# A two-layer transformer and a mixture of experts on one core: eleven step durations changed in the planner's table

## The chip, the cores and the metric

One Trainium2 chip, one of its cores. The metric is the time of one execution of the whole program on that core, in microseconds (us). Three runs of the kernel before give a median of 3349.57 us (3342.55 to 3351.56).

## What is computed

Eight sequences of 512 tokens of width 256 (`x`) and as many contexts go through two layers. The reference, cut to what matters:

```python
# layer 0, 16 heads of 16, quantised attention; _fq rounds to 8 bits
h1 = _ln(x);  x = _attn(h1, h1, a1_*) + x            # stage 0
h2 = _ln(x);  x = _attn(h2, context, a2_*) + x       # stage 1
h3 = _ln(x);  a, g = split(h3 @ ff_w1 + ff_b1)       # stage 2
x = a * gelu(g) @ ff_w2 + ff_b2 + x
# in _attn: out = einsum(_fq(softmax(_fq(q) @ _fq(k).T * SCALE)), _fq(v)) @ wo + bo
# layer 1, exact attention
x = _layernorm(x + _attn(x, x, x, sa_*, causal=True))        # stage 3
x = _layernorm(x + _attn(x, enc, enc, ca_*, causal=False))   # stage 4
x = _layernorm(x + _moe(x))     # 8 experts, 2 per token     # stages 5, 6, then experts
```

## The kernel before

`build` (its last part) runs two programs after each other: `transformer`, the stages 0 to 6 for all eight batches, and `experts`, the mixture of experts, the last normalisation and the output. The change touches the first alone.

The transformer is cut into some 12,000 **steps**, each a tuple `(kind, B, s, n)`: a kind of work, the batch, the stage, a number. `program_steps` (L245) names for each step what it must follow. `ON` (L93) puts each kind on one engine. `program_order` (L498) is a list scheduler that runs while the kernel is being built: it plays the steps through with planned durations, takes again and again the step that could begin first (within `AHEAD`, 0.05 us, the one with the longest way to the end, `to_end`), and writes the list `ORDER`. Every engine then issues its own steps in the order of that list and waits on semaphores for what each needs. So the planned durations change no instruction and no semaphore rule; they set only the order in which each in-order engine takes its steps, which bank of PSUM (6 or 7) a projection gets, and where fillers go.

The planned durations are `TAKES` (L111), `takes` (L159) for kinds with several sizes, `LANDS` for DMAs from issue to landing, `HOP` and `TAIL` for what lies between engines. **Fillers**: where the plan leaves PE idle for `WARM_GAP` (0.4 us) or more and a bank is idle, `program_order` puts in steps `W` (L1462), products of an identity that nobody reads, so that PE does not stand still.

The kinds that the text speaks of:

- Quantised attention (stages 0 and 1), 32 units of two heads each: `S` scores on PE (L1564, two products), `M` row maximum on DVE (L1293), `nb` (L1296), `E` exponential on ACT (L1429, two per unit), `R` reciprocal on DVE (L1299), `Q` on POOL (L1096), `T` eight transposes on PE (L1572), `ev` on DVE (L1305), `AV` on PE (L1584).
- Exact attention (stages 3 and 4): `A` scores on PE (L1595) whose row maxima `am` DVE takes (L1313), `ms` and `MT` (L1604) and `mt` (ACT, L1437), which put the maxima as rows under q; then `B` the shifted scores (L1617), `E2` their exponential on ACT (L1448, L1450), `AV2` (L1634), `n1` (DVE). `A` and `B` read q and k as stacks of bfloat16 parts, `kst` and `qst`. A stack is made by a round trip through DRAM: `spk` / `spq` split on POOL (L1104 to L1110), `psk` / `psq` store the parts (SP, L970), `pkk` / `pkq` load them again in six DMAs (SP, L983). Each stack comes in two halves: the first is needed by `A` number 0, the second by `A` number 32.
- Projections and feed-forward: `xT`, `cT` transposes (L1503), `k`, `q` (L1519), `v` (L1515), `y` (L1532), `g` and `w` (L1542, 16 steps each), `z` (L1553). `dg` drains `g` on ACT (L1411), and `ge` is the GELU over all of it, two instructions on ACT (L1416); every `w` waits for it, by `("ge", B, 2, 0)` in its step.
- Weights stream through a ring of six pieces of 256 KB (`wring`, L910). SP issues the load of a piece at the place in `ORDER` where the last reader of the piece six before it stands. So a new order of projections also moves DMA issues on SP's queue, which is one line with the stores and loads of the stacks.

The exact attention of one batch runs beside the quantised attention and feed-forward of the next ones. Batches 1 to 6 repeat one pattern. Time in that pattern, for the texts below: stage 0 of batch 3 with the feed-forward of batch 2, then stage 3 of batch 2, then stage 1 of batch 3, then stage 4 of batch 2.

Of the kernel before, what the change touches and what calls it, by code (L numbers as in the profile page):

```python
# [71 lines left out]
def place_taken(B):  # L72
# [36 lines left out]
ROUTING_OPENS = ("A", 6, 3, 0)  # L109
AHEAD = 0.05  # L110
TAKES = {"LR": 0.5, "rT": 0.49, "dr": 0.66, "rL": 1.95, "rl": 0.64, "rx": 0.25, "rm": 1.4, "ry": 0.25, "ri": 3.6, "rP": 0.36, "rp": 1.4, "sc": 1.1,  # L111
# [3 lines left out]
         "ki": 0.46, "qi": 0.45, "vi": 0.4, "psk": 0.5, "psq": 0.5, "pkk": 2.7, "pkq": 2.7,  # L115
         "dy": 0.6, "g": 0.88, "dg": 0.62, "ge": 6.4, "w": 0.9, "dw": 0.65, "z": 0.97, "dz": 0.6,
         "bi": 0.7, "gb": 1.53, "ST": 0.5, "LX": 0.5, "LC": 0.5, "st": 0.88, "rs": 1.4, "xn": 0.53}
TAIL = {"PE": 0.13, "DVE": 0.08, "ACT": 0.08, "POOL": 0.0, "SP": 0.0}
HOP = {"PE": 0.12, "DVE": 0.06, "ACT": 0.06, "POOL": 0.09, "SP": 0.3}
# [1943 lines left out]
```

## Time and profile before

| | |
|---|---|
| median of three runs | 3349.57 us |
| the profiled execution's own time | 3340.18 us |
| its span | 3338.4 us, 59062 instructions |
| PE / DVE / ACT / POOL busy | 2940.4 / 2165.5 / 1959.5 / 1625.8 us (88 / 65 / 59 / 49%) |
| mean granted TensorE clock | 0.947 |
| DMA | 344.05 MB, 103 GB/s over the span |
| number of GELU table loads and GELUs on ACT | 8 and 16 |

The busy time of PE is modelled and counts overlapping matmuls, so PE looks busier than it is. "issue" as a releaser means that the engine waited for nothing that the profile shows: a DMA's semaphore is often such a case. The transformer ends at about 2745 us, and the experts take the rest.

### The profile page before, as it was taken

What the parts mean: (1) busy time and instruction counts of PE and PEld (TensorE: products, weight loads), DVE (VectorE), ACT (ScalarE), POOL (GpSimd) and SP (SyncE); (2) the same over time, 40 slices, a digit from 0 to 9 for tenths busy, and PEclk for the clock granted to TensorE, in tenths of its full rate; (3) what the DMA queues carried; (4) which work ended last, traced back from release to release, by engine and by line L of the source; (5) the groups of instructions that cost most, each with busy time, mean ns of one, the idle gap of its engine ahead of it and who ended that gap; (6) DMA issues with size and microseconds to landing.
All of it is one profiled execution on the core that took longest, in us unless ns stands there. A gap on an engine that the chain in (4) does not pass through costs nothing. (4 is left out here: it accounts for less than half of the span.)

```text
span 3338.4 us, 59062 instructions
## 1 busy us (share of the span) xinstructions
PE 2940.4 (88%) x19111; PEld 1705.4 (51%) x19111; DVE 2165.5 (65%) x4580; ACT 1959.5 (59%) x4178; POOL 1625.8 (49%) x2835
## 2 busy tenths in 40 slices
PE   6888999899998898989999989987988859999991
PEld 3445443544454354435443544454435229999991
DVE  4887796788678787967896788778656511111115
ACT  3666667576758676675767576757354404444442
POOL 4665572675367366726763664457435321111115
PEclk9999999999999999999999999997999879999996
DMA  3002331422142214303320422141433239999995
GB/s 95 17 23 65 65 63 32 86 61 56 34 96 51 51 42 92 71 26 83 71 54 24 90 44 61 29 86 36 107 79 85 46 83 326 326 325 327 324 327 164
DMA packets 295832, 344.05 MB, mean 103 GB/s; under 512 B 33262, under 2 KB 273006, under 8 KB 295328
## 3 DMA queue, kind: packets, MB, share of 16 engines
q1 hardware_dynamic: 287376, 323.35, 36.7%
q0 software_dynamic: 6480, 17.58, 1.6%
q8 instruction: 133, 2.18, 0.3%
q14 instruction: 115, 0.94, 0.1%
q10 hardware_dynamic: 1728, 0.01, 0.0%
HBM read 291.50 MB, written 51.23 MB: 103 GB/s over the span
## 5 line engine op out<-in xcount | busy, mean ns | idle before, releaser
L1429 ACT ACTIVATE probs<-ps,nbias,sc 128x512 f32<-128x512 f32 x1024 | 789.9, 777 | 270.1 <-DVE nbias L1296 223.1
L1096 POOL TENSOR_SCALAR pq<-probs,rstep 128x512 f16<-128x512 f32 x1024 | 709.7, 693 | 232.9 <-PE ps L1572 147.9
L1313 DVE TENSOR_REDUCE m<-ps 128x1 f32<-128x512 f32 (+3 forms) x1024 | 560.7, 582 | 249.4 <-PE ps L1598 128.8
L1293 DVE TENSOR_REDUCE nmax<-ps 128x2 f32<-128x1024 f32 x512 | 620.3, 1212 | 85.9 <-PE ps L1564 85.4
L1595 PE MATMUL ps<-kst,qst 96*128 96x512 bf16 (+3 forms) x1024 | 330.2, 354 | 77.2 <-issue 39.9
L1305 DVE TENSOR_SCALAR big<-ps 128x1024 bf16<-128x1024 f16 x512 | 348.1, 680 | 61.6 <-PE ps L1572 60.1
L1906 ACT ACTIVATE hT<-moe_ps,e_b 128x128 f32<-128x128 f32 x568 | 208.3, 367 | 281.4 <-PE moe_ps L1860 242.2
L1572 PE MATMUL ps<-id,pq 128*128 128x128 f16 x4096 | 328.1, 226 | 47.5 <-DVE big L1305 40.5
L1617 PE MATMUL ps<-qst,kst 108*128 108x512 bf16 (+3 forms) x1024 | 304.5, 351 | 66.2 <-ACT big L1448 29.5
L1572 PEld LDWEIGHTS ps<-id,pq 128*128 128x128 f16 x4096 | 258.5, 100 | 190.7 <-issue 124.6
L1448 ACT ACTIVATE big<-ps 128x512 f32<-128x512 f32 (+3 forms) x640 | 272.9, 482 | 134.4 <-PE ps L1620 83.4
L1812 POOL DMA_INDIRECT rows_out<-yb,words x71 | 69.9, 984 | 472.8 <-DVE yb L1991 472.8
L1984 DVE COPY words<-moe_in 128x3 uint32 x71 | 12.0, 169 | 432.4 <-PE moe_ps L1882 432.4
L1542 PE MATMUL ps<-xT,wring 128*128 128x512 f32 x512 | 270.5, 636 | 0.3
L1860 PEld LDWEIGHTS moe_ps<-moe_bT,e_w 128*128 128x128 f32 x2272 | 266.1, 193 | 5.5 <-issue 2.0
L1860 PE MATMUL moe_ps<-moe_bT,e_w 128*128 128x128 f32 x2272 | 266.5, 276 | 1.8 <-DMA e_w<-in_L_xattn_e_w_dram 1.8
L1882 PE MATMUL moe_ps<-e_w,hT 128*128 128x256 f32 x1136 | 256.8, 380 | 0.0
L1595 PEld LDWEIGHTS ps<-kst,qst 96*128 96x128 bf16 x1024 | 98.1, 99 | 303.2 <-DVE m L1313 178.1
L1564 PE MATMUL ps<-kmask,qi 32*128 32x512 bf16 x1024 | 203.7, 397 | 40.2 <-ACT probs L1429 27.7
L1462 PE MATMUL ps<-idb 128*128 128x512 bf16 x777 | 215.9, 393 | 26.0 <-DVE sc L1144 19.8
L1634 PE MATMUL ps<-big,v_f 128*32 128x512 f32 (+3 forms) x2048 | 234.5, 535 | 2.6 <-ACT big L1448 0.8
L1882 PEld LDWEIGHTS moe_ps<-e_w,hT 128*128 128x128 f32 x1136 | 210.8, 191 | 25.3
(219 smaller groups left out, 4671.8 us busy)
## 6 DMA issues: line engine op xcount, KB each, us to landing
e_w<-in_L_xattn_e_w_dram SPq DMA_DIRECT2D x142, 1024.0 KB, 7.5
wring<-in_L_xattn_ff_w_dram SPq DMA_DIRECT2D x96, 256.0 KB, 2.8
parts<-parts_sb SPq DMA_DIRECT2D x64, 384.0 KB, 2.6
kst<-parts SPq DMA_DIRECT2D x192, 128.0 KB, 4.5
qst<-parts SPq DMA_DIRECT2D x192, 128.0 KB, 5.0
moe_in<-rows_in SPq DMA_DIRECT2D x71, 140.0 KB, 2.6
xn<-in_ctx_dram SPq DMA_DIRECT2D x16, 512.0 KB, 3.8
got<-rows_out SPq DMA_DIRECT2D x16, 512.0 KB, 6.8
```

The lines of the kernel that those rows point to most:

```text
L1096: nc.gpsimd.tensor_scalar(pq[:, u % 2, h, :], probs[:, u % 2, h, :], rstep[:, u % 2, h:h + 1], HALF_ROUND, ALU.mult, ALU.add).then_inc(SIG ...
L1293: nc.vector.tensor_reduce(nmax[:, n % 2, :], ps[:, a:a + 2, :], AX.X, ALU.max, negate=True).then_inc(SIG["M"], 1)
L1305: nc.vector.tensor_scalar(probs_t[:, g % 2, 2 * p:2 * p + 2, :, t * P:(t + 1) * P], PT, -HALF_ROUND, WMAX, ALU.add, ALU.min).then_inc(SIG[ ...
L1313: nc.vector.tensor_reduce(m32[:, g % 2, t, h:h + 1], bank(("A", B, s, n))[:, 0:width], AX.X, ALU.max, negate=True).then_inc(SIG["am"], 1)
L1429: nc.scalar.activation(probs[:, u % 2, h, :], ps[:, BANKS[("S", B, s, u)][h], :], ACT.Exp, bias=nbias[:, u % 2, h:h + 1], scale=sc[:, s:s ...
L1448: last = nc.scalar.activation(ex[:, half, h, j, i0:N], ps[:, from_, i0:N], ACT.Exp, scale=SCALE)
L1542: last = nc.tensor.matmul(bank(e), wt[:, k, (f % 2) * P:(f % 2 + 1) * P], xT[:, k, :], start=(k == 0), stop=(k == KT - 1))
L1572: last = nc.tensor.transpose(PT[:, h, j, :], pq[:, n % 2, h, j * P:(j + 1) * P], id16[:, :])
L1595: last = nc.tensor.matmul(bank(e)[:, 0:width], qst[0:PAIR_ROWS, head, t * P:(t + 1) * P], kst[0:PAIR_ROWS, head, 0:width], start=True, sto ...
L1617: last = nc.tensor.matmul(dst[:, i0:N], kst[0:rows_, head, jt * P:(jt + 1) * P], qst[0:rows_, head, i0:N], start=True, stop=not causal(s))
L1860: last = nc.tensor.matmul(ps[:, HIDDEN_BANK[f % banks], 0:BLOCK], w1[:, slot, k, f * P:(f + 1) * P], bT[:, slot % 2, k, :], start=(k == 0) ...
L1882: last = nc.tensor.matmul(ps[:, 2 + 2 * slot + s, 0:D], hT[:, slot, f, s * P:(s + 1) * P], w2[:, ws, f, :], start=(f == 0), stop=(f == FT ...
```

## The change

Eleven numbers of `TAKES` are replaced: `S`, `M`, `T`, `MT`, `xT`, `cT`, `dc`, `k`, `q`, `ki` and `ge`. Nothing else differs in the source.

```diff
-         "W": 0.22, "S": 0.38, "M": 1.14, "nb": 0.14, "E": 0.76, "R": 0.08, "T": 0.46, "ev": 0.61, "AV": 0.23, "do": 0.6,
-         "ms": 1.1, "MT": 0.32, "mt": 0.95, "n1": 0.92, "n2": 0.6, "n3": 0.62,
-         "xT": 0.49, "dT": 0.66, "cT": 0.44, "dc": 0.5, "k": 0.88, "q": 0.88, "v": 0.97, "dv": 0.6, "dV": 0.6,
-         "ki": 0.46, "qi": 0.45, "vi": 0.4, "psk": 0.5, "psq": 0.5, "pkk": 2.7, "pkq": 2.7,
-         "dy": 0.6, "g": 0.88, "dg": 0.62, "ge": 6.4, "w": 0.9, "dw": 0.65, "z": 0.97, "dz": 0.6,
+         "W": 0.22, "S": 0.32, "M": 1.17, "nb": 0.14, "E": 0.76, "R": 0.08, "T": 0.5, "ev": 0.61, "AV": 0.23, "do": 0.6,
+         "ms": 1.1, "MT": 0.1, "mt": 0.95, "n1": 0.92, "n2": 0.6, "n3": 0.62,
+         "xT": 0.52, "dT": 0.66, "cT": 0.55, "dc": 0.48, "k": 0.92, "q": 0.92, "v": 0.97, "dv": 0.6, "dV": 0.6,
+         "ki": 0.6, "qi": 0.45, "vi": 0.4, "psk": 0.5, "psq": 0.5, "pkk": 2.7, "pkq": 2.7,
+         "dy": 0.6, "g": 0.88, "dg": 0.62, "ge": 3.73, "w": 0.9, "dw": 0.65, "z": 0.97, "dz": 0.6,
```

The new `ORDER` holds the same work with 779 fillers where there were 777. Of the 4304 steps of PE that are no fillers, 3251 stand at another place than before, most of them by a few places; of DVE's 3584 steps 1785 do, of ACT's 2200 steps 1194, of POOL's 1832 steps 860.

SP's queue, batch 2, before the first `A` of stage 3. `wring` is a weight piece, `parts<-parts_sb` a store of parts (`psk` or `psq`), `kst<-parts` and `qst<-parts` the loads of the stacks (`pkk`, `pkq`). Before:

```order
L910 DMA wring<-in_L_xattn_a_wo_dram 128x2x256
L970 DMA parts<-parts_sb 128x3x512 x2
L910 DMA wring<-in_L_xattn_ca_wq_dram 128x2x256
L983 DMA kst<-parts 16x8x512 x6
L910 DMA wring<-in_L_xattn_ca_wv_dram 128x2x256
L983 DMA qst<-parts 16x8x512 x6
L910 DMA wring<-in_L_xattn_a_wq_dram 128x2x256
L910 DMA wring<-in_L_xattn_ca_wk_dram 128x2x256
L970 DMA parts<-parts_sb 128x3x512
```

Now:

```order
L910 DMA wring<-in_L_xattn_a_wo_dram 128x2x256
L970 DMA parts<-parts_sb 128x3x512
L983 DMA kst<-parts 16x8x512 x6
L910 DMA wring<-in_L_xattn_a_wq_dram 128x2x256
L970 DMA parts<-parts_sb 128x3x512
L910 DMA wring<-in_L_xattn_ca_wq_dram 128x2x256
L983 DMA qst<-parts 16x8x512 x6
L910 DMA wring<-in_L_xattn_ca_wk_dram 128x2x256
L910 DMA wring<-in_L_xattn_ca_wv_dram 128x2x256
L970 DMA parts<-parts_sb 128x3x512
```

The store and the load of k's stack now stand ahead of the store of q's parts, and between that store and the load of q's stack there is one weight piece, where there were two pieces and the load of k's stack.

ACT around the GELU of batch 2 (`uT<-uT`). `uT<-ps,ffb` is `dg`, `qst<-ps` is `mt`, `probs` is `E`, `big` is `E2`. Before:

```order
L1411 ACTIVATE uT<-ps,ffb 128x512
L1416 ACT_TABLE_LOAD
L1416 ACTIVATE uT<-uT 128x2048 x2
L1437 ACTIVATE qst<-ps 12x1024
L1429 ACT_TABLE_LOAD
L1429 ACTIVATE probs,rsum<-ps,nbias,sc 128x512
L1448 ACTIVATE big<-ps 128x512
L1429 ACTIVATE probs,rsum<-ps,nbias,sc 128x512
L1448 ACTIVATE big<-ps 128x512
L1429 ACTIVATE probs,rsum<-ps,nbias,sc 128x512
```

Now:

```order
L1448 ACTIVATE big<-ps 128x512
L1429 ACTIVATE probs,rsum<-ps,nbias,sc 128x512
L1448 ACTIVATE big<-ps 128x512
L1437 ACTIVATE qst<-ps 12x1024
L1429 ACTIVATE probs,rsum<-ps,nbias,sc 128x512
L1448 ACTIVATE big<-ps 128x512
L1429 ACTIVATE probs,rsum<-ps,nbias,sc 128x512 x2
L1411 ACTIVATE uT<-ps,ffb 128x512
L1416 ACT_TABLE_LOAD
L1416 ACTIVATE uT<-uT 128x2048 x2
L1448 ACT_TABLE_LOAD
L1448 ACTIVATE big<-ps 128x512
```

The GELU with its two table loads stood ahead of both `mt` of the last head group of stage 4; now it stands behind both, behind six `E` and behind four `E2`. On PE the last two `g` steps moved from ahead of the second `S` to behind the first `T`, and the first `w` from behind the fourth `S` to behind the seventh.

## Rows read from the trace of the kernel before

**Rows 1.** Windows: stretch, length; busy PE, PEld, DVE, ACT, POOL; clock, DMA share, GB/s.

```profile
0.00:2745.00 2745.00, 2423.68 (x15561) 1218.43 (x15561) 2033.15 (x4199) 1713.71 (x3506) 1514.96 (x2716) 0.95 0.27 60
...
850.40:1160.60 310.20, 282.91 (x1867) 143.62 (x1866) 245.45 (x482) 212.24 (x435) 179.82 (x327) 0.97 0.29 60
850.40:871.00 20.60, 13.37 (x55) 5.38 (x54) 11.18 (x22) 18.55 (x32) 6.92 (x13) 0.75 0.05 12
...
946.50:953.50 7.00, 1.04 (x6) 0.38 (x5) 0.00 (x0) 3.23 (x7) 5.28 (x7) 0.78 1.14 195
...
1004.30:1029.30 25.00, 21.02 (x159) 9.30 (x160) 20.62 (x41) 22.95 (x56) 20.63 (x37) 0.93 0.18 43
```

**Rows 2.** Waits of PE, transformer only: total us, times, longest.

```profile
PE ps L1595 <- issue: 39.9, 10, 8.1
...
PE ps L1617 <- ACT qst L1437: 28.3, 11, 4.1
```

**Rows 3.** Timeline of PE around the first score product of batch 2.

```profile
945.31 1.88 PE L1519 MATMUL ps<-xT,wring 128*128 128x512 f32 x4
953.15 0.26 PE L1595 MATMUL ps<-kst,qst 96*128 96x128 bf16 x1 [5.96 <-issue]
```

**Rows 4.** Timeline of DVE, the same place.

```profile
953.56 0.51 DVE L1313 TENSOR_REDUCE m<-ps 128x1 f32<-128x128 f32 x2 [7.25 <-PE ps L1598]
```

**Rows 5.** Timeline of SP's queue, the same place.

```profile
934.44 1.49 SPq L970 DMA_DIRECT2D parts<-parts_sb  x2
...
938.65 2.79 SPq L983 DMA_DIRECT2D kst<-parts  x6
...
942.01 2.78 SPq L983 DMA_DIRECT2D qst<-parts  x6
```

**Rows 6.** Timeline of ACT around the GELU of batch 2.

```profile
848.15 0.69 ACT L1411 ACTIVATE uT<-ps,ffb 128x512 f32<-128x512 f32 x1 [1.89 <-PE ps L1542]
848.86 1.28 ACT L1416 ACT_TABLE_LOAD   x1
850.15 3.71 ACT L1416 ACTIVATE uT<-uT 128x2048 f32<-128x2048 f32 x2
853.89 1.02 ACT L1437 ACTIVATE qst<-ps 12x1024 bf16<-12x1024 bf16 x1
854.92 1.28 ACT L1429 ACT_TABLE_LOAD   x1
```

**Rows 7.** Timeline of PE, the same place.

```profile
850.45 0.39 PE L1564 MATMUL ps<-kmask,qi 32*128 32x512 bf16 x2
854.96 0.61 PE L1617 MATMUL ps<-qst,kst 108*128 108x512 bf16 x1 [4.12 <-ACT qst L1437]
857.72 0.58 PE L1617 MATMUL ps<-qst,kst 108*128 108x512 bf16 x1 [2.15 <-ACT big L1448]
...
866.61 0.39 PE L1617 MATMUL ps<-qst,kst 108*128 108x512 bf16 x1
```

**Rows 8.** SP's queue before the first score product of another stage.

```profile
769.38 0.37 SPq L970 DMA_DIRECT2D parts<-parts_sb  x1
771.91 2.70 SPq L983 DMA_DIRECT2D qst<-parts  x6
```

**Rows 9.** Page, DMA issues: count, KB each, median us from issue to landing.

```profile
qst<-parts SPq DMA_DIRECT2D x192, 128.0 KB, 5.0
```

**Rows 10.** SP's queue, second stacks of batch 2.

```profile
963.72 0.38 SPq L970 DMA_DIRECT2D parts<-parts_sb  x1
969.73 2.83 SPq L983 DMA_DIRECT2D qst<-parts  x6
```

**Rows 11.** Instructions by line and form: count, busy us, mean ns.

```profile
L1429 ACT ACTIVATE probs<-ps,nbias,sc 128x512 f32<-128x512 f32 x1024 | 789.9, 777 | 270.1 <-DVE nbias L1296 223.1 <-POOL pq L1096 44.7
...
L1448 ACT ACTIVATE big<-ps 128x512 f32<-128x512 f32 x256 | 153.4, 599 | 75.0 <-PE ps L1617 47.3 <-PE ps L1620 24.2 <-PE ps L1634 1.3
```

**Rows 12.** Timeline of PE at the start of stage 1 of batch 3.

```profile
1010.79 0.39 PE L1564 MATMUL ps<-kmask,qi 32*128 32x512 bf16 x2 [2.30 <-ACT probs L1429]
```

## The prediction

> **What bounds the kernel now.** Read the windows first [rows 1]. The transformer takes the first 2745 us of the span; the change cannot touch the rest. Batches 1 to 6 repeat a pattern of 310.20 us, in which DVE is busy 245.45 us, ACT 212.24, POOL 179.82, and PE 282.91 by a modelled figure that counts overlaps. No engine fills the pattern alone: PE and DVE take turns as the bound, and what a new order can win is the stretches where both stand. Two of them show. In 850.40 to 871.00 DVE works 11.18 us of 20.60 and the granted clock is 0.75. In 946.50 to 953.50 DVE works not at all, PE 1.04 us of 7.00, at a share of 1.14 on the DMA engines. A third is milder: 1004.30 to 1029.30 has DVE at 20.62 of 25.00.
>
> The waits of PE [rows 2] name them. `A` waited ten times, 39.9 us, for something that the profile does not show. `B` waited eleven times, 28.3 us, for the rows of maxima that ACT copies (`mt`), 4.1 us at most.
>
> The first: PE ends q's projection for stage 3, then stands 5.96 us before the first `A` [rows 3], and DVE stands 7.25 us [rows 4]. SP's queue says why [rows 5]: the parts of k and q are stored from 934.44 on, k's stack is loaded from 938.65, q's only from 942.01, over 2.78 us, and `A` starts when its last piece is there, at 953.15. Of the ten waits six are this one, in batches 1 to 6 (the other four are smaller or at the two ends). They leave 39.9 as an upper bound for all, and six times 5.96 is 35.8; I use 36.
>
> The second: ACT loads a table for GELU (1.28 us), runs it (3.71), copies maxima (1.02), then loads the table for the exponential (1.28) [rows 6]. PE issued its `S` at 850.45, waits 4.12 for the copy and 2.15 for an `E2` behind the second load [rows 7]. This too comes once in each of six batches.
>
> **The change part by part.** No instruction but fillers is added or removed, so every term is a wait that goes, comes or moves. Each is for one batch of the pattern and counts six times; the sum is made against the profiled execution's 3340.2 us.
>
> *q's stack.* In the new list SP stores q's parts behind k's stack load, and one weight piece stands between that store and the load of q's stack. The nearest row of such a chain alone is that of another stage: store at 769.38, load of q's stack from 771.91 to 774.61 [rows 8], and 5.0 us for a piece to land [rows 9], so 10.2 us from store to landing, where here it took from about 935.2 (the second store of the pair at 934.44) to 953.15, 18 us [rows 3, 5]. Against that stands the work that PE has between the store and the first `A`. Going through the new list it is four `S`, four `T`, three `v`, two `q` steps and one `k`, 8.6 us; before it was 10.6, and 10.6 + 6.0 is 1.4 short of the 18: that much PE waits for other things there. Now 10.2 - 8.6 - 1.4 is nearly nothing; as the k stack and one more piece are on the same DMA engines, I leave a wait of 1.5. Minus 4.5, times six: **-27**. Bounds: the wait goes wholly (-36), or nothing is won (0; the rival below goes past it).
>
> *The second half of q's stack*, needed by the 33rd `A`. Before, its parts were stored at 963.72 and, behind k's stack on the DMA engines, took until 969.73, where the load began [rows 10]; with 2.83 us of issuing and 5.0 to land [rows 9] it was there at about 977.6, 24.4 us after the first `A` and ahead of its use by little. Nothing in the new list makes this chain shorter, but the 33rd `A` now stands some 4.5 us of PE work nearer to the first (a `y` pair, `B` steps and one `AV2` moved behind it). DVE's row maxima slow PE there and give part of it back, so I take a new wait of 1.5 us: **+9**. Bounds 0 and +4 each (+24).
>
> *The GELU.* The new value 3.73 is the two instructions' 3.71 us without the two table loads of 1.28 beside them; the old 6.4 was 3.71 + 2 x 1.28 = 6.27 with both [rows 6]. So the planner now thinks ACT free 2.6 us before it is. By hand from rows, counted from the second `S` of the new stage: ACT does six `E` of 0.78, four `E2` of 0.60 [rows 11], one `mt` of 1.02 and one `dg` of 0.69, 8.8 us with 0.8 of waiting; then 6.27 us of GELU and loads, then the `E2` that frees the bank of the next `B`: that `B` comes at +16.5. Before it was 866.61 - 850.45 = 16.2 [rows 7]. The long wait is not removed, it moves from the 25th `B` to the 30th. Until then PE has done two `g`, a `T` and a `cT` more and two `w` less. Then ACT owes six `E` and four `E2`, 7.1 us, for which PE has 4.6 us of work, as the first `w` comes late. I set 2.0 us slower: **+12**. Bounds: 1.5 faster (-9), when PE catches up while DVE bounds it; 4 slower (+24).
>
> Here a page speaks against the change. The trace shows a load of 1.28 us, and the first GELU starts 0.01 us after it [rows 6]. The Trainium skill, page "ScalarE: Activation LUTs", section "What ACT_TABLE_LOAD costs", gives 1283 ns for the load and about 1380 ns more for a drain, 2.66 us for each switch; by that the two switches would be 5.3 us, and the planner would be 2.7 us further off in each batch, some 16 us over six, which would take this sum to about nothing. The trace agrees with the load and shows no drain ahead of the GELU, so the sum goes by 1.28.
>
> *Start of stage 1.* PE waited 2.30 us for an `E` at 1010.79 [rows 12], and DVE's idle share from 1004.30 to 1029.30 is 4.4 us in 25. In the new list the products of q and the `E` stand ahead of the normalisation on POOL, and k's projection of stage 4 (four steps) stands later, where fillers stood. DVE is then the bound and can win at most the idle time above that of its packed stretches: I take 1.5 us: **-9**. Bounds 0 and 3 (-18).
>
> *Everything else* (the other thousands of neighbours that changed places): nothing, because DVE or PE has no gap over 1 us beside them. *Two more fillers*: nothing, at most 0.4 us each, and they stand where PE idles. First and last batch: nothing, with 8 us to either side in the range; there fewer fillers stand ahead of the last stage 4, and chains of single steps set the time.
>
> **The sum**: -27 + 9 + 12 - 9 = -15 us, 3325 us for the execution profiled. That execution is 9.4 us under the median of the runs. Scaled to the median: 3349.6 - 15 = **3334.5 us**. A measurement of this kernel can tell some 0.3%, 10 us, from no change, so the forecast is just past that line.
>
> **The rivals.**
>
> *Slower: q's stack lands as late as it did, counted from its use.* Mechanism: the load of q's stack is issued with 6.0 us of PE work ahead of the first `A`, before it had 6.5, and the store of q's parts queues behind k's stack, as it did there (6.0 us from 963.72 to 969.73, where the same store alone took 2.5 [rows 8, 10]). For it: exactly this queueing stands in the trace. Against: in the new list k's stack is issued some 5 us of PE work before q's store, so most of it is through. If the chain from store to landing is 16 us instead of 10.2, it is shortened only by the 2 us that the cover lost, and the wait stays at 6.0. From there on it decides: with nothing won at the first `A` the rest is 9 + 12 - 9 = +12, **3362 us**.
>
> *Same: the GELU eats the win.* ACT's backlog is not made good before the next stage, since PE is full from 871 to 946: 4 us per batch instead of 2, or the second half of q's stack waits 3 us. Then -15 + 12 = -3, **3347 us**. A drain of 1.38 us at each switch, which no row shows, would end here too (-15 + 6 x 2.7 = +1, 3350 us): chance 0.03 of the 0.27; the rule is the Trainium skill's, as above.
>
> *Same, in another way*: the order is not what bounds the pattern; whatever wait is taken from PE, DVE's 245 us with its own chains give it back. Against it: in both big holes DVE stands too. It gives 3350 us.
>
> **How the numbers follow.** Forecast and its like (faster by more than 10 us): 0.52. Slower by more than 10 us, the first rival above all: 0.21. The cases that end within 10 us: 0.27 (the GELU 0.17, the drain 0.03, the order without effect 0.07). The best corner that I believe (first wait gone, GELU even) is 15 + 9 + 12 + 6 = 42 us: 3307, with a little for the ends 3306. The upper end is the first rival with 0.8 us more at each second half, 3366. The range leaves out 2 in 10.
>
> **What would show it.** In the profile after: the wait of `A` on "issue" well under 39.9 us in total, under 20, with a hole in DVE ahead of the first `A` of under 3 us; on SP's queue k's stack load ahead of q's store. At the 33rd `A` a wait that was not there. ACT: the two table loads and the GELU behind six `E`, and one wait of `B` on `big` of about 5 us instead of 4.12 on `qst` and 2.15; the sum of waits of `B` on `qst` down by 25 us and on `big` up by more. It is wrong if the pattern of 310.2 us is not 2 to 3 us shorter, if `A`'s waits stay, or if the time changes mainly in the first batch or the last 400 us.

## The result, and the profile after

The changed kernel takes **3412.12 us** (median of four runs, 3406.90 to 3432.70); the kernel before, run beside it, 3346.06 (3341.36 to 3351.56). The ratio is **1.0202**, 95% interval 1.0183 to 1.0221: 66 us slower. The forecast was 3334.5, and its range ended at 3366. The execution profiled took 3417.22 us at a span of 3415.4 and a clock of 0.930, against 3340.18 and 0.947 before.

The windows of the changed kernel, columns as in [rows 1]:

```profile
0.00:2825.00 2825.00, 2484.01 (x15563) 1238.67 (x15563) 2054.03 (x4200) 1719.73 (x3506) 1523.89 (x2716) 0.93 0.27 58
...
868.90:1193.70 324.80, 292.03 (x1867) 146.34 (x1866) 249.23 (x482) 212.81 (x434) 181.11 (x327) 0.94 0.28 58
1193.70:1514.60 320.90, 290.57 (x1868) 144.59 (x1867) 249.10 (x482) 212.89 (x434) 181.25 (x327) 0.95 0.28 58
```

The same work, 1867 matmuls and 482 instructions of DVE, takes 321 to 325 us per batch where [rows 1] had 310.20. ACT is busy as long as before, DVE 4 us longer. PE is busy 8 to 9 us longer with as many matmuls, at a clock of 0.94 to 0.95 instead of 0.97, and stands 30 to 33 us instead of 27. So the loss is a few us in which PE stands, and more in which it works at the lower clock around them.

PE's waits in the transformer of the changed kernel, columns as in [rows 2]:

```profile
PE ps L1617 <- ACT big L1448: 53.4, 69, 3.2
PE ps L1564 <- ACT probs L1429: 40.8, 80, 3.6
...
PE ps L1595 <- issue: 33.3, 11, 9.4
...
PE ps L1617 <- ACT qst L1437: 9.5, 16, 1.1
...
PE ps L1595 <- DMA qst<-parts: 4.9, 5, 1.5
```

Against [rows 2], `B`'s waits for `mt` fell from 28.3 to 9.5 us, and `A`'s for its stack only from 39.9 to 33.3. What grew are the waits for `E2`, 53.4 us, and for `E`, 40.8, both ACT's: these two rows stood at 29.5 and 27.7 us before.

ACT around the GELU of batch 2, which answers to [rows 6]:

```profile
879.66 0.69 ACT L1411 ACTIVATE uT<-ps,ffb 128x512 f32<-128x512 f32 x1 [0.23 <-PE ps L1542]
880.36 1.28 ACT L1416 ACT_TABLE_LOAD   x1
881.66 3.71 ACT L1416 ACTIVATE uT<-uT 128x2048 f32<-128x2048 f32 x2
885.38 1.28 ACT L1448 ACT_TABLE_LOAD   x1
886.68 0.60 ACT L1448 ACTIVATE big<-ps 128x512 f32<-128x512 f32 x1
```

And PE beside it, which answers to [rows 7]:

```profile
883.66 0.61 PE L1572 MATMUL ps<-id,pq 128*128 128x128 f16 x8 [2.08 <-DVE big L1305]
887.42 0.58 PE L1617 MATMUL ps<-qst,kst 108*128 108x512 bf16 x1 [3.15 <-ACT big L1448]
888.78 0.59 PE L1617 MATMUL ps<-qst,kst 108*128 108x512 bf16 x1 [0.78 <-ACT big L1448]
```

The block of 6.3 us on ACT is as foreseen, and the waits at it, 2.08 + 3.15 us, are even shorter than the 4.12 + 2.15 of [rows 7]. Whoever looks only at the wait that the change moves finds nothing wrong. The windows show where the loss is:

```profile
870.00:882.00 12.00, 8.35 (x45) 3.82 (x40) 7.46 (x15) 11.08 (x21) 4.06 (x9) 0.86 0.09 23
882.00:895.00 13.00, 6.46 (x31) 1.41 (x31) 4.93 (x9) 12.09 (x20) 4.47 (x8) 0.63 0.01 1
895.00:931.00 36.00, 35.20 (x193) 18.18 (x190) 27.76 (x52) 19.82 (x47) 15.74 (x30) 0.99 0.11 30
```

For 25 us ACT is full (11.08 of 12, 12.09 of 13) and PE has 14.8 us of work; then for 36 us PE is full and ACT has 19.8. The work that could have covered the first stretch stands in the second.

**Where the time went.** From the starts of named steps, mean of batches 1 to 5, in us. "w" is the time from the first `S` of stage 0 to the first `w`; the columns after it are the stretches S(0,0) to S(0,16), on to the first `A` of stage 3, to S(1,0), to S(1,16), to the next S(0,0), and their sum.

```
kernel                             w    S0-S16   to A   to S1  S1-S16  to S0    sum
before                           14.3    53.8    50.9    51.0    42.1  112.6   310.4
changed                          28.7    62.9    46.9    55.4    45.9  111.6   322.7
e1  changed, ge 6.4              12.4    53.4    47.1    52.0    46.0  112.5   311.0
e2  before, ge 3.73              28.8    62.6    51.5    53.0    42.8  114.2   324.1
e3  before, MT 0.1               14.3    54.1    51.6    52.4    43.0  112.8   314.0
e4  before, landing 5.0          12.2    57.1    43.5    48.8    42.8  114.4   306.7
e5  before, w held               24.2    57.7    50.7    53.5    43.1  112.6   317.6
e6  before, no table loads       11.7    51.3    50.9    51.3    42.5  112.5   308.5
e7  changed, no table loads      26.1    60.1    46.8    55.3    45.0  111.6   318.8
e8  e1, landing 5.0              12.1    58.1    44.6    52.1    43.6  111.5   310.0
e9  e1, context early            12.4    53.7    46.5    52.6    41.8  115.8   310.4
e10 changed, GELU pinned         11.6    53.1    46.6    52.0    43.7  112.8   308.2
e11 before, landing 4.0          12.7    54.6    45.5    50.0    43.2  114.4   307.7
e12 e9, landing 4.0              12.6    54.9    44.7    50.8    43.1  114.6   307.9
e13 changed, ge 4.2              20.2    57.9    46.6    56.2    45.3  112.0   318.1
e14 e10, landing 4.5             11.5    57.3    44.7    51.6    41.1  114.6   309.3
```

The table is made of five batches. Between the two profiled executions lie 77 us, and the same step starts divide them: five times 12.3, 62 us, from S(2,0,0) to S(7,0,0), the stretches of the table; 11 us from S(1,0,0) to S(2,0,0) (321.1 and 331.9), where the exact attention of batch 0 runs; and 4 us behind them. The 11 us of the first batch stay with the GELU put back (333.6 in e1, 334.4 in e10) and do not come with ge alone (323.1 in e2): they belong to the other ten values, not to the GELU.

A second caution: the borders of the stretches are steps, and a new order also moves work over them. In the changed kernel two `g` that stood ahead of S(0,0) stand behind it, and in e4 S0-S16 holds 13 steps of `z` where it held 7. Only the sum is free of that. The profiled execution of the kernel before lies 5 to 16 us under its own medians (3346 to 3357 in the sets below), so differences of 1 to 1.5 us a batch between two rows of this table are not resolved; where they matter the ratio of the runs decides.

### The profile page after: what moved, and what is told of

It reads as the page before. It is cut to its first block and busy times, and to the rows that moved or that the text cites. A ratio compares the mean times of both kernels' runs of the same rounds, so it can differ in the third digit from the quotient of the medians.

```text
span 3415.4 us, 59059 instructions
## 1 busy us (share of the span) xinstructions
PE 3001.9 (88%) x19113; PEld 1726.5 (51%) x19113; DVE 2186.1 (64%) x4580; ACT 1965.8 (58%) x4178; POOL 1633.7 (48%) x2835
## 5 line engine op out<-in xcount | busy, mean ns | idle before, releaser
L1595 PE MATMUL ps<-kst,qst 96*128 96x512 bf16 (+3 forms) x1024 | 330.7, 354 | 65.9 <-issue 33.3
L1617 PE MATMUL ps<-qst,kst 108*128 108x512 bf16 (+3 forms) x1024 | 314.5, 362 | 73.3 <-ACT big L1448 53.4
L1572 PEld LDWEIGHTS ps<-id,pq 128*128 128x128 f16 x4096 | 265.6, 102 | 179.3 <-issue 95.2
L1634 PE MATMUL ps<-big,v_f 128*32 128x512 f32 (+3 forms) x2048 | 250.8, 576 | 11.9 <-ACT big L1448 10.9
L1564 PE MATMUL ps<-kmask,qi 32*128 32x512 bf16 x1024 | 206.9, 403 | 52.7 <-ACT probs L1429 40.8
L1462 PE MATMUL ps<-idb 128*128 128x512 bf16 x779 | 222.9, 402 | 25.7 <-DVE sc L1144 19.8
L1092 POOL TENSOR_TENSOR rstep<-rinv,inv_step 128x2 f32<-128x2 f32 x512 | 103.1, 201 | 294.5 <-DVE rinv L1299 285.8
```

The lines of the kernel that those rows point to most:

```text
L1572: last = nc.tensor.transpose(PT[:, h, j, :], pq[:, n % 2, h, j * P:(j + 1) * P], id16[:, :])
L1595: last = nc.tensor.matmul(bank(e)[:, 0:width], qst[0:PAIR_ROWS, head, t * P:(t + 1) * P], kst[0:PAIR_ROWS, head, 0:width], start=True, sto ...
L1617: last = nc.tensor.matmul(dst[:, i0:N], kst[0:rows_, head, jt * P:(jt + 1) * P], qst[0:rows_, head, i0:N], start=True, stop=not causal(s))
```

## The experiments

Each ratio is to the kernel before, run beside it. The theories after the result: the loss is a few single places, the GELU's above all; against it, that any new order of this list loosens the cover everywhere.

**e1: ge put back.**

```diff
-         ... "ge": 3.73, ...
+         ... "ge": 6.4, ...
```

> The changed kernel with one value put back: ge 6.4 instead of 3.73. ACT then takes the GELU right behind dg 7 and ahead of the first E of the next stage, as before, while k of stage 4 stays six units of S later, as in the changed kernel. Theory P (the loss is in single places, the GELU's the largest): the stretch from S(B+1,0,0) to S(B+1,0,16) goes back from 61 to about 54 us, some 8 us x 7 batches, so about 3356 us; the start of stage 1 stays 4 us too long. Theory Q (the loss belongs to no place: any new order loosens the cover everywhere and the clock falls): 3395 to 3410.

Measured: 3352.63 us, ratio 1.0002 (0.9989 to 1.0015). The stretch S0-S16 is back at 53.4 us, the start of stage 1 stays at 46.0, both as the theory of single places has it. The other ten values together are worth nothing, within 5 us. That is a net: by the profiled executions they win 3.8 us a batch on the way to the first `A`, and lose 3.9 at the start of stage 1 and 12 in the first batch. The mean clock does not tell the time by itself: the twelve executions of e1 show 0.932 to 0.939 and those of the kernel before beside it 0.943 to 0.946, and the times are the same.

**e2: ge changed alone, in the kernel before.**

```diff
-         ... "ge": 6.4, ...
+         ... "ge": 3.73, ...
```

> The kernel before with one value changed: ge 3.73. The GELU moves behind four of the first E steps, w behind the sixth S; k of stage 4 stays where it was. Theory P: 8 us x 7 batches on top, about 3400 us, all of it between S(B+1,0,0) and S(B+1,0,16). Theory Q: 3350 to 3360, since the rest of the order is still the old one. My forecast's own term (+2 us a batch) would give 3360.

Measured: 3410.91 us, 1.0175 (1.0162 to 1.0188). One number makes 61 us, and its first stretch, 62.6 us, is within 0.3 us that of the changed kernel. The theory that any new order loses falls with e1, the forecast's +2 us with this one.

**e3: MT changed alone.**

```diff
-         "ms": 1.1, "MT": 0.32, ...
+         "ms": 1.1, "MT": 0.1, ...
```

> The kernel before with one value changed: MT 0.1. The GELU stays ahead of the first E; k of stage 4 moves from the third to behind the ninth S of stage 1. Theory P: start of stage 1 (S 0 to S 16) 4 to 5 us longer in each batch, about 3376 us, the rest unchanged. Rival: k late costs nothing there, since fillers and ACT's queue set the pace, and the 4 us of the changed kernel come from something else: 3346 us.

Measured: 3357.22 us, 1.0023 (1.0013 to 1.0033): 8 us slower, where theory P had 3376 us and the rival no loss. S1-S16 is 43.0 us. k of stage 4 is now as late as in the changed kernel (22.4 us after S(1,0), changed 24.1, before 10.6) and costs about 1 us there, not 4. The rival is nearer: k's lateness alone is not the +3.8 us.

**e4: the landing time of the stacks.**

```diff
-LANDS = {..., "psk": 2.2, "psq": 2.2, "pkk": 2.2, "pkq": 2.2, ...}
+LANDS = {..., "psk": 5.0, "psq": 5.0, "pkk": 5.0, "pkq": 5.0, ...}
```

> The kernel before with the landing time of the four stack DMAs planned at 5.0 us instead of 2.2; no duration changed. k and q of stage 3 move two to three units of S earlier. Theory P: the wait ahead of A(B,3,0), 6.0 us in the kernel before, falls under 1.5 us and nothing else moves much: 3346 - 5 x 7 = about 3311 us. Rival: k and q taken earlier leave PE without cover at the end of stage 0, or the first S units lose it: 3340 to 3355.

Measured: 3324.01 us, 0.9929 (0.9916 to 0.9942): faster than both kernels. Waits of `A` in it:

```profile
PE ps L1595 <- DVE m L1313: 32.5, 115, 0.7
...
PE ps L1595 <- DMA qst<-parts: 2.5, 3, 1.1
...
PE ps L1595 <- issue: 1.7, 1, 1.7
```

39.9 us on "issue" have become 1.7. The rival is partly right too: 7.4 us a batch are won on the way to the first `A` and 2.2 behind it, and 3.3 lost in S0-S16 and 1.8 in the last stretch; into S0-S16 the new order moves six steps of `z`. That is why 26 us came and not 35.

**e5: w held back, the GELU left in its place.** Also "ge" 4.5 and `E(B+1,0,3)`, the fourth exponential, behind `ge`; in the list that these make, the GELU of batches 1 to 6 stands ahead of the first `E` and the first `w` behind the seventh `S`, where e2 has it.

```diff
-                step("w", ..., ("ge", B, 2, 0), k and ("w", B, 2, 2 * f))
+                step("w", ..., ("ge", B, 2, 0), k and ("w", B, 2, 2 * f),
+                     f == 0 and k == 0 and B + 1 < NBATCH and ("S", B + 1, 0, 4))
```

> The kernel before with the GELU kept right behind dg 7 and ahead of the first E, as it was there, but with w forbidden to start until S(B+1,0,4) is done, so that the first w comes behind the sixth S, where the kernel with ge 3.73 alone has it (before: behind the third). Nothing of ACT's work is moved to speak of. Theory C (w and z are the PE work that covers ACT's long queue of E and E2, and their delay is the loss, wherever the GELU stands): S 0 to S 16 takes 60 to 62 us and the kernel 3390 to 3410. Theory B (the loss is ACT's block of 6.3 us falling in the middle of the running E pipeline instead of ahead of it): 54 to 55 us, and 3346 to 3355.

Measured: 3381.87 us, 1.0075 (1.0057 to 1.0093): between the two. S0-S16 is 57.7 us: 3.9 of e2's 8.8 us. Theory B, which gave at most 55, falls as the whole story; theory C gave 60 to 62 and is right in kind, too large in size. The windows of batch 3 from the first `S` to the first `w`, and from there to S 16, say where e2 differs. The kernel before, then e5, then e2:

```profile
848.00:862.30 14.30, 7.07 (x41) 2.28 (x40) 5.90 (x11) 14.00 (x19) 3.05 (x6) 0.74 0.06 19
862.30:901.90 39.60, 39.54 (x218) 18.99 (x216) 32.71 (x60) 27.59 (x65) 19.88 (x39) 0.96 0.10 28
```

```profile
860.00:883.90 23.90, 15.48 (x90) 5.72 (x86) 14.00 (x25) 23.27 (x42) 8.71 (x17) 0.71 0.04 12
883.90:917.20 33.30, 32.98 (x178) 16.51 (x174) 25.59 (x45) 17.61 (x42) 14.59 (x27) 1.00 0.11 32
```

```profile
862.60:888.90 26.30, 16.50 (x85) 5.50 (x84) 12.06 (x22) 23.61 (x40) 8.22 (x16) 0.77 0.05 15
888.90:923.70 34.80, 34.80 (x186) 17.00 (x184) 27.26 (x49) 19.01 (x46) 15.28 (x30) 0.98 0.12 31
```

In all three PE is full from the first `w` on (39.54 of 39.60, 32.98 of 33.30, 34.80 of 34.80), and before it ACT is nearly so, PE to a half or two thirds at a clock of 0.71 to 0.77. The first stretch is where time is lost: it grows by 9.6 and 12.0 us, and the second, with fewer matmuls left for it, shrinks by only 6.3 and 4.8. In e5 ACT is full to the last (23.27 of 23.90); in e2 it stands 2.7 us of the window, in a hole of 3.16 us ahead of its first `E` that begins before the window:

```profile
864.59 0.78 ACT L1429 ACTIVATE probs<-ps,nbias,sc 128x512 f32<-128x512 f32 x1 [3.16 <-DVE nbias L1296]
```

That is the time in which the first `S`, its row maxima and its bias pass through PE and DVE. ACT has nothing to do then, and in the kernel before the GELU stood there. Of the 4.9 us between e5 and e2 this hole may be a part; another is that e2 also has three `g` steps behind S 0 (0.88 us planned for each), which e5 has ahead of it. No run parts the two.

**e6 and e7: no table loads**, in the kernel before and in the changed one. Both leave out the GELU, so the output differs.

```diff
-                        nc.scalar.activation(part, part, ACT.Gelu)...
+                        nc.scalar.activation(part, part, ACT.Identity)...
```

> The kernel before with ACT.Identity in place of ACT.Gelu in L1416, so that the GELU is left out and with it the two table loads around it (the output differs). The loads are 2 x 1.28 us of ACT at a place where PE waits: 8 x 2.57 = 21 us less at most, about 3328 us; 3346 if something else ends those waits.

> The changed kernel with ACT.Identity in place of ACT.Gelu in L1416, so that the two table loads around each GELU are gone and 3.73 us is what it takes (the output differs). If the uncounted loads are the damage (theory L), this comes within 10 us of the run without loads of the kernel before. Theory C: the planner's place is a bad one even when its price is right, since it puts w and z behind ACT's queue either way; the difference to the other run stays over 40 us, this one about 3385 us.

Measured: 3339.53 us, 0.9955 (0.9940 to 0.9971), and 3388.83 us, 1.0110 (1.0093 to 1.0127). The two instructions are as long as GELU was (1904 ns in e7, 1902 in the changed kernel), so only the loads are gone. In S0-S16 that is 2.5 us in the one and 2.8 in the other, about 2 x 1.28. Over the whole kernel it is 15 us in e6 and, from the two ratios, some 31 in e7, around the 20.5 us that the sixteen loads last. The two runs stand 49 us apart, where the kernels with loads stand 66. So theory L falls as the main cause: 3.73 is the true time in e7, and the planner's place for it is still bad.

By the Trainium skill (page "ScalarE: Activation LUTs", section "What ACT_TABLE_LOAD costs"), which gives 2.66 us for each switch, an estimate for the two switches is 5.3 us. The rows of this case do not bear out the part beside the load: ACT's next instruction starts 0.02 us after each of the two loads at 880.36 and 885.38, and the stretch became shorter by the loads alone.

**e8: ge put back, and landing 5.0.** The edits of e1 and e4 in the changed kernel.

```diff
-         ... "ge": 3.73, ...
+         ... "ge": 6.4, ...
-LANDS = {..., "psk": 2.2, "psq": 2.2, "pkk": 2.2, "pkq": 2.2, ...}
+LANDS = {..., "psk": 5.0, "psq": 5.0, "pkk": 5.0, "pkq": 5.0, ...}
```

> The changed kernel with ge back at 6.4 and the landing of the four stack DMAs planned at 5.0 us instead of 2.2, that is, the run with ge put back (1.0002 of the kernel before) plus the change that alone gave 0.9929. If the two are additive: 3326 us, the wait ahead of A(B,3,0) under 1 us. If the ten new durations gained only by closing part of that same wait, which the landing time closes as well, their losses at the start of stage 1 (4 us a batch) stay and it is slower than that: 3335 to 3350.

Measured: 3346.23 us, 0.9967 (0.9954 to 0.9981). Not additive, as the second case had it. But the reason that I gave for it fails: against e4 the largest loss is 3.3 us between the first `A` and S(1,0), and in S1-S16 it is 0.8, not 4.

**e9: the context early**, in e1.

```diff
-            step("S", B, s, u, *(...), free)
+            step("S", B, s, u, *(...), free, u == 0 and s == 1 and B and ("cT", B - 1, 4, 1))
```

> The run with ge put back (e1), and in its planner one more condition: S(B+1,1,0) behind cT(B,4,1). That puts cT 1 of the context, and with it k of stage 4 (four matmul groups, 4 us of PE), back where the kernel before has them, k behind the third S of stage 1 instead of the ninth, and 11 fillers instead of 4 to 5 into S 0 to S 16. Theory K (the ten other values lose 4 us a batch at the start of stage 1 because its PE cover is gone and the granted clock falls there a second time, 15 to 25 us in, to 0.77 and 0.67): S 0 to S 16 goes from 46.0 to about 42 us, the clock stays at 1.0 in that stretch, and the kernel takes 3349 - 4 x 7 = about 3322 us. Rival: the same work is only moved out of that stretch into the next ones (y of stage 3 and AV2), as the run with MT alone suggests (+0.9 us): 3345 to 3352.

Measured: 3356.24 us, 0.9998 (0.9987 to 1.0010). Windows of e1, S(3,1,0) to S(3,1,16) and its part from 15 to 25 us:

```profile
1013.00:1058.80 45.80, 38.03 (x289) 19.61 (x285) 38.35 (x72) 35.24 (x87) 33.34 (x58) 0.89 0.21 39
1028.00:1038.00 10.00, 8.59 (x59) 3.74 (x58) 9.24 (x22) 8.28 (x22) 7.95 (x15) 0.83 0.00 0
```

and of e9:

```profile
1014.80:1056.60 41.80, 35.46 (x284) 17.03 (x283) 35.15 (x69) 35.60 (x87) 33.35 (x59) 0.92 0.19 36
1029.80:1039.80 10.00, 7.98 (x62) 3.40 (x61) 7.83 (x16) 9.90 (x24) 8.42 (x14) 1.00 0.10 28
```

The stretch is 4.2 us shorter and the clock in its part holds at 1.00, exactly as theory K says, and the kernel is no faster: the stretch behind it grew by 3.3 us. The low clock went there too. The next 40 us or so, in e1 and in e9:

```profile
1058.80:1098.50 39.70, 37.86 (x283) 19.91 (x283) 35.49 (x74) 30.59 (x71) 33.93 (x63) 1.00 0.34 63
1056.60:1100.50 43.90, 39.13 (x273) 22.23 (x271) 38.71 (x77) 30.56 (x70) 33.70 (x60) 0.92 0.32 63
```

Theory K falls, the rival holds. The loss, in work and in clock, was moved over a border that I had drawn.

**e10: all eleven values, the GELU pinned.**

```diff
-                step("E", B, s, 2 * u + h, ("nb", B, s, u), ...)
+                step("E", B, s, 2 * u + h, ("nb", B, s, u), 2 * u + h == 2 and s == 0 and B and ("ge", B - 1, 2, 0), ...)
```

> The changed kernel with all its eleven durations, ge 3.73 among them, and one more condition in the planner: E(B+1,0,2) behind ge(B). The GELU so comes right behind dg 7 and ahead of the first E again, with its price left at 3.73. If its place alone is the loss: S 0 to S 16 about 54 us, the same 3350 us as with ge put back. If the price does harm elsewhere too (it shortens every chain that passes over the GELU, and so changes whom the planner prefers): 3365 to 3400.

Measured: 3341.76 us, 0.9963 (0.9950 to 0.9975). The price stays wrong, only the place is forced (the GELU of batches 1 to 6 is ahead of the first `E` again), and the whole loss is gone and a little more. Its windows, as above:

```profile
860.70:872.30 11.60, 5.09 (x28) 1.79 (x27) 5.30 (x9) 11.47 (x16) 2.20 (x4) 0.72 0.02 6
872.30:913.80 41.50, 41.44 (x233) 20.50 (x230) 34.69 (x64) 28.70 (x68) 21.51 (x42) 0.95 0.09 26
```

The stretch to the first `w` is 11.60 us. The 12 us that it wins are not the ten values' alone, since with ge 6.4 they win nothing (e1); the kernel before with 3.73 and the pin, which would part them, was not run.

**e11 and e12: landing 4.0**, in the kernel before and in e9.

```diff
-LANDS = {..., "psk": 2.2, "psq": 2.2, "pkk": 2.2, "pkq": 2.2, ...}
+LANDS = {..., "psk": 4.0, "psq": 4.0, "pkk": 4.0, "pkq": 4.0, ...}
```

> The kernel before with the landing of the four stack DMAs planned at 4.0 us (5.0 gave 0.9929, 2.2 is the kernel before). The wait ahead of A(B,3,0), 8.8 us from S 31 before and 2.2 with 5.0, should be 3 to 4 us; what 5.0 cost on the other side (S 0 to S 16 up by 3.3 us, A(B,4,0) to A(B,4,63) up by 4.3) should be less. If these two trade evenly: 3325 to 3330 us; if the cost on the other side is mostly avoided: 3310 to 3320.

> The ten other new durations with ge at 6.4, the context kept early as in the run with S(B+1,1,0) behind cT(B,4,1), and the stack DMAs planned at 4.0 us. If the measured durations are worth something once the two bad places are out: under the run with landing 4.0 alone, 3300 to 3315 us. If the ten durations are neutral: the same as that run. If their orders conflict (849 fillers and 3346 us with landing 5.0, where additivity gave 3326): over it, 3330 to 3345.

Measured: 3337.19 us, 0.9943 (0.9929 to 0.9958), and 3336.16 us, 0.9953 (0.9935 to 0.9971). In e11 S0-S16 costs 0.8 us instead of 3.3 and the way to `A` gains 5.4 instead of 7.4: the two trade evenly. In e12 the ten values add nothing.

**e13: ge 4.2** in the changed kernel, which puts the GELU behind the second `E` and the first `w` behind the sixth `S` (the expectation counts from 0).

```diff
-         ... "ge": 3.73, ...
+         ... "ge": 4.2, ...
```

> The changed kernel with ge 4.2 instead of 3.73: the GELU stands behind the second E, in the middle of the started pipeline but earlier, and the first w behind the fifth S and T 2 (changed kernel: behind the sixth S and T 2, with the GELU behind the sixth E; with ge 6.4: behind the second S). Theory C, read as a dose: of the runs so far S 0 to S 16 is 53 to 54 us where w starts 12 to 14 us after S 0 and 62.6 to 62.9 where it starts 28.8 after, 0.6 us for each us. Here w starts at 22 to 25 us, so 58 to 60 us, and the kernel 3375 to 3395. Theory B (any GELU behind the first E costs the whole): over 62 us and 3405 to 3415; if only a GELU behind four or more E hurts: 54 us and 3350.

Measured: 3387.09 us, 1.0120 (1.0106 to 1.0135). `w` starts at 20.2 us, S0-S16 is 57.9. So a GELU in the middle of the pipeline does not cost the whole, and the price grows with the delay of `w`: 14.3, 20.2, 24.2 and 28.8 us (before, e13, e5, e2) give 53.8, 57.9, 57.7 and 62.6. But e13 starts `w` 4 us ahead of e5, and its stretch is no shorter. Two things can be behind that: the GELU's place itself, and two `g` steps (0.88 us planned for each) that stand behind S 0 in e13 and ahead of it in e5. How the shares divide stays open. The delay of `w` also sets the stretch only where the work in it is the same: e4, e8 and e14 start `w` at 11.5 to 12.2 us and take 57.1 to 58.1, with 13 steps of `z` in it for 7 or 8.

**e14: e10 with landing 4.5.**

```diff
-LANDS = {..., "psk": 2.2, "psq": 2.2, "pkk": 2.2, "pkq": 2.2, ...}
+LANDS = {..., "psk": 4.5, "psq": 4.5, "pkk": 4.5, "pkq": 4.5, ...}
```

> The changed kernel's eleven durations, E(B+1,0,2) behind ge(B) (alone 0.9963 of the kernel before) and the stack DMAs planned at 4.5 us. Additive with the landing time's 0.993: 3305 to 3315. As in the earlier combinations, where two repairs of the same wait did not add: 3325 to 3345.

Measured: 3346.17 us, 0.9996 (0.9982 to 1.0010), just past the upper end of the second case. Two repairs that win alone, 0.9963 and, at 4.0 and 5.0, 0.9943 and 0.9929, give nothing together; S0-S16 is 57.3 us, as in e4, where the stack DMAs are planned long too.

## Why the prediction was wrong

**The GELU: the step that failed.** I took +2.0 us a batch with bounds of -1.5 and +4; S0-S16 measured +9.1 in the changed kernel and +8.8 with ge alone, and over the whole pattern the changed kernel lies 11.7 us a batch above e1, its like with ge put back. Its count was right (the long wait moves to a later `B`; +16.5 us foreseen, and that `B` starts 18.5 us after S 0 and 16.9 after S 1), and its conclusion was not. I compared the wait before and after, and wrote "two `g` more and two `w` less" for PE. What the GELU releases is not two `w` but all sixteen, and the sixteen `z` behind them: a long stock of PE work that does not stand in ACT's queue of `E` and `E2`. Until the first `w` ACT is the full engine and PE is not. That stretch grew from 14.3 to 28.7 us, and the stretch in which PE is full shrank only from 39.5 to 34.2. e1, e2 and e10 show that the place does it, and e5 that the delay of `w` alone, with the GELU left where it was, makes 3.9 of e2's 8.8 us in S0-S16. The rest of it is argued and not shown: the hole at ACT's start (3.16 us in e2) and the `g` steps that came behind S 0 are two candidates.

**The mispriced loads were a red herring.** I took the missing 2.57 us of table loads for the planner's error. e7 has no loads and still loses 49 of the 66 us against e6. By the rule of `to_end`, the old value of 6.4 made the chain through the GELU look longer, and `g` 14 and 15 were taken ahead of the first `S`; with 3.73 the last `g` starts 9.7 us after S 0 instead of 1.1 before it.

**q's stack** was sized well as a net, 4.0 us a batch won up to the first `A` for 4.5 forecast, and wrongly as a chain. PE and DVE there, which answer to [rows 3, 4], and SP's queue, to [rows 5, 10]:

```profile
978.37 0.26 PE L1595 MATMUL ps<-kst,qst 96*128 96x128 bf16 x1 [3.92 <-issue]
```

```profile
978.78 0.50 DVE L1313 TENSOR_REDUCE m<-ps 128x1 f32<-128x128 f32 x2 [3.91 <-PE ps L1598]
```

```profile
963.31 0.40 SPq L970 DMA_DIRECT2D parts<-parts_sb  x1
...
969.69 2.69 SPq L983 DMA_DIRECT2D qst<-parts  x6
...
989.59 0.86 SPq L970 DMA_DIRECT2D parts<-parts_sb  x1
995.79 3.02 SPq L983 DMA_DIRECT2D qst<-parts  x6
```

The order on SP is as said, but from the store to the first `A` it is 15.1 us, not the 10.2 that I had from another stage. That is nearly the 16 us of the rival, and the load stands 6.4 us behind the store, as the rival's 6.0. The wait shrank even so, since PE had 11.1 us to do meanwhile and not 10.0: that a wrong chain and a wrong cover gave nearly the right net was luck in part. Over batches 1 to 6 the wait at the first `A` fell from 6.1 us to 2.8 in the mean (3.92 is its largest), not to 1.5. "issue" is at 33.3 in all, not under 20, but 9.4 of that is the first `A` of batch 0 and only 16.7 the six that the term was about. In e1 and e10, with the GELU in place, no wait over 0.8 us is left at these six, so there the wait goes wholly, which was my lower bound.

**The second half of the stack**: +1.5 forecast, and the stretch from the first `A` to S(1,0) measured +4.4, past the bound of 4. But it is not the wait that I forecast: PE shows none at the 33rd `A` in batches 1 to 6. The load stands at 995.79, 17.4 us after the first `A`, where [rows 3, 10] have 16.6, and is issued by 998.81; the 33rd `A` of batch 2 starts at 1003.92, straight behind the product ahead of it. The stretch parted at the 33rd `A`, first before and then changed:

```profile
953.10:979.00 25.90, 24.50 (x172) 16.23 (x173) 22.49 (x58) 7.45 (x14) 8.70 (x18) 0.92 0.61 106
979.00:1004.20 25.20, 25.18 (x226) 13.79 (x223) 19.22 (x45) 17.70 (x39) 14.85 (x31) 1.00 0.28 85
```

```profile
978.30:1003.80 25.50, 22.85 (x137) 12.55 (x138) 19.96 (x49) 5.88 (x10) 6.42 (x13) 0.83 0.57 104
1003.80:1035.50 31.70, 31.27 (x262) 18.55 (x260) 21.85 (x54) 22.21 (x51) 19.49 (x40) 0.98 0.22 67
```

Ahead of the 33rd `A` stand 35 matmuls fewer, at a clock of 0.83 instead of 0.92, and that part is no longer than before; behind it stand 36 more with PE full, and that part is 6.5 us longer. Among the work that moved behind are the four `y` steps of stage 0. In e1 and e10 the same ten values make +1.0, and e13 has it all: most of this too hangs on the late GELU. Why, no run took apart.

**Start of stage 1**: -1.5 forecast, +3.8 measured, the sign wrong. But e9 takes it back and wins nothing. As far as the runs show it was a matter of the border, and neither my term nor its opposite should have stood in the sum.

**The first batch** was forecast at nothing, with 8 us to either side, and measured +11 us. Its first `A` waits 9.4 us instead of 5.2, and the largest part, 7 us, comes in the start of its stage 1, S(1,1,0) to S(1,1,16) (39.7 and 46.7 us). It belongs to the ten other values (e1, e10); which of them, no run says.

**The rest**, forecast at nothing, is -1.0 us a batch. The sum by what was measured: 5 x (-4.0 + 4.4 + 9.1 + 3.8 - 1.0) = +62, and 11 for the first batch and 4 at the end make 77, where I had -15. Of the rivals, "the GELU eats the win" was right about what is lost, ACT's backlog, and with 4 us a batch about a third of its size; it did not see the stock of `w` and `z` either. The slower rival had the right chain on SP and was not the cause.

## What to carry to other kernels

When a step is moved in a list, don't price the wait that moves with it. Ask what the step releases, how much of it, and which engine's slack that work was filling; then take the windows from the stage's start to the first released step, and look whether one engine is full there while another, with work still to come, is not. A planner's costs are also its priorities: a truer duration can shorten the chain that rightly stood first, so pin what must come first as a condition (e10) rather than trust a number to do it. And judge a term at the end of the pattern, not at a border inside it (e9), and the first batch by itself.

## What the runs showed of the hardware

A table switch on ACT took the time of its load and no more on ACT: without the two loads of 1.28 us the stretch is 2.5 and 2.8 us shorter, the GELU's load starts within 0.02 us of the end of the instruction ahead of it, and the first GELU 0.02 us after the load. What a switch costs the kernel depends on its place: the sixteen loads last 20.5 us, and leaving them out won 15 us in one order and some 31 in the other.

The granted clock fell where PE stood or was half idle: in the windows ahead of the first `w` its mean is 0.71 to 0.77, a mix of time at 2.4 and at 1.2 GHz, and 0.95 to 1.00 in those behind it. In the changed kernel 1867 matmuls of a batch take 8 to 9 us more of PE's busy time than as many before. But a lower mean clock need not cost time: e1 ran at 0.932 to 0.939 as fast as the kernel before at 0.943 to 0.946.

A store and the load that reads it back took 15.1 us from the store's issue to the use in one place, and 18 in another with the same sizes and k's store and load in the same queue; in a third they took 10.2 by an estimate from issue times and the median landing. No single number plans it, yet raising the planned landing from 2.2 to 5.0 us gave 0.9929, the lowest ratio of all kernels run here.
